# First layer of a four-layer kernel: skip term on TensorE, state faded by GpSimd, last convolution tap by ScalarE

## The reference, cut to what matters

```
zxbcdt = x @ W_in.T                      # z: 512, xBC: 512 + 128 + 128, dt: 64
xBC = silu(causal_conv(xBC, conv_w))     # 4 taps, each channel by itself
dt = softplus(dt_raw + dt_bias); a = dt * -exp(A_log); cum = cumsum(a) in the chunk
Yd = tokens of the same chunk: (C B^T * exp(cum_i - cum_j) * dt_j) @ xs
S_next = S * exp(cum_last) + sum_j exp(cum_last - cum_j) dt_j B_j xs_j
Yoff = exp(cum) * (C @ S)
y = Yd + Yoff + D * xs                   # D: one factor for each head
yz = y * silu(z)
out = (yz * rsqrt(mean(yz^2) + 1e-5) * norm_w) @ W_out.T
```

## Time and profile before

| | |
|---|---|
| runs | 1543.8, 1531.72, 1533.39 us; median 1533.39 us |
| profiled execution | span 1528.5 us from the first to the last instruction; the time of this execution by itself is not listed, the runs shown are 3 to 15 us above the span |
| busy, share of the span | PE 1297.5 us (85%), DVE 916.0 us (60%), ACT 550.5 us (36%), POOL 363.7 us (24%) |
| mean granted TensorE clock | 0.919 of full speed |
| first layer | about 0 to 606 us of the span |

### The profile page before, as it was taken

How to read it: one execution, slowest core, us unless ns; L and a number is a source line. 1 busy time by engine, 2 the same in 40 slices (tenths; PEclk the granted TensorE clock), 3 DMA queues, 4 the chain that set the end, 5 groups by cost and what they waited for, 6 DMA issues and landing times. The chain is left out here.

```text
span 1528.5 us, 21650 instructions
## 1 busy us (share of the span) xinstructions
PE 1297.5 (85%) x7315; PEld 808.2 (53%) x7315; DVE 916.0 (60%) x1809; ACT 550.5 (36%) x917; POOL 363.7 (24%) x346
## 2 busy tenths in 40 slices
PE   5676898898889776889999998999767889999996
PEld 3445545564555455556666745445453456544554
DVE  6776576656675775443312458889877453556344
ACT  2465256635553651222222242442422313233310
POOL 3167113211224142620040002211137000000043
PEclk9886998999899878989999999999958899999998
DMA  9242203220312220400000070000002110112123
GB/s 356 62 114 84 58 24 110 75 67 22 113 41 59 50 91 25 161 11 1 1 0 0 0 248 1 0 1 1 0 19 88 32 31 28 39 39 63 56 62 97
DMA packets 72081, 88.86 MB, mean 58 GB/s; under 512 B 19174, under 2 KB 55334, under 8 KB 71337
## 3 DMA queue, kind: packets, MB, share of 16 engines
q1 hardware_dynamic: 65836, 70.78, 15.1%
q0 software_dynamic: 6144, 16.79, 3.4%
HBM read 61.14 MB, written 26.38 MB: 57 GB/s over the span
## 5 line engine op out<-in xcount | busy, mean ns | idle before, releaser
L397 PE MATMUL l_banks<-l_xnT,all_region_a 128*128 128x512 f32 x288 | 130.2, 605 | 0.0
L913 POOL TENSOR_TENSOR all_region_b<-all_region_b,l_lc 128x512 f32<-128x512 f32 x64 | 89.1, 1412 | 119.8 <-DMA all_region_b<-l_lc_rows 119.5
L1966 PE MATMUL l_banks<-l_xnT,mid_region_c 128*128 128x512 f32 (+1 forms) x192 | 89.4, 615 | 10.8 <-DVE l_xnT L2182 10.8
L397 PEld LDWEIGHTS l_banks<-l_xnT,all_region_a 128*128 128x128 f32 x288 | 54.9, 194 | 62.3 <-issue 61.1
L397 PE MATMUL l_banks<-all_region_b,l_xp 128*32 128x32 f32 x2048 | 35.4, 213 | 48.5 <-DVE all_region_b L1182 43.1
L397 PE MATMUL l_banks<-all_region_a,all_xa 128*128 x234 | 71.6, 436 | 3.8 <-DVEq L1241 2.7
L745 ACT ACTIVATE all_region_b<-all_region_b 128x512 f32<-128x512 f32 x64 | 69.4, 1084 | 4.9 <-PE l_banks L397 0.7
L397 PEld LDWEIGHTS l_banks<-all_region_b,l_xp 128*32 128x32 f32 x2048 | 29.2, 125 | 70.6 <-DVE all_region_b L1182 37.4
L1182 DVE TENSOR_TENSOR all_region_b<-all_region_b,l_cbd 128x512 f32<-128x512 f32 x64 | 56.4, 882 | 16.6 <-ACT all_region_b L745 12.6
L1966 PEld LDWEIGHTS l_banks<-l_xnT,mid_region_c 128*128 128x128 f32 (+1 forms) x192 | 35.1, 188 | 57.1 <-issue 45.3
L2849 POOL TENSOR_TENSOR l_rstd<-l_moments,all_neg_half 128x4 f32<-128x4 f32 x12 | 12.4, 1033 | 219.6 <-DVE l_moments L2909 218.6
(11 more groups left out here) (473 smaller groups left out, 2845.1 us busy)
## 6 DMA issues: line engine op xcount, KB each, us to landing
all_region_b<-l_lc_rows SPq DMA_DIRECT2D x256, 64.0 KB
all_xa<-slots_in SPq DMA_DIRECT2D x39, 128.0 KB, 2.1
slots_out<-all_xa SPq DMA_DIRECT2D x39, 128.0 KB, 1.7
mid_vector_rows<-slots_in SPq DMA_DIRECT2D x39, 128.0 KB, 2.1
slots_out<-all_region_a SPq DMA_DIRECT2D x39, 128.0 KB, 1.7
slots_in<-l_xp SPq DMA_DIRECT2D x4, 1024.0 KB, 12.9
all_region_a<-l_gate_up SPq DMA_DIRECT2D x1, 4096.0 KB, 15.3
all_x<-x SPq DMA_DIRECT2D x4, 512.0 KB, 5.7
```

What stands on the lines that cost most here:

```text
L397: return nc.tensor.matmul(out, lhsT, rhs, start=start, stop=stop, **kw)
L913: nc.gpsimd.tensor_tensor(bc[:, k, :, :], bc[:, k, :, :], spread(lc[:, c, heads], 1, BLK), ALU.subtract).then_inc(dd_ready.sem, 1)
L1966: return nc.tensor.matmul(out, lhsT, rhs, start=start, stop=stop)
```

## The change

It moves work of the first layer between engines and leaves the arithmetic the same but for the order of additions:

- **Last tap.** After evicting a convolution block to `pre`, ACT evicts it a second time into `xbc`, scaled by the last tap's weight; DVE's convolution is then three multiply-adds on top and no first multiplication.
- **Skip term.** ACT makes four diagonal 128x128 matrices of D from the identity once a group (`skips`, in the unused `pre[:, 4]`), behind the wait for the shared expert and ahead of `place`. PE multiplies them with the chunk of `xbc` (`skipped`, four f32 matmuls of 128x128) ahead of strip 1; they open the accumulation in the bank of y, and `assemble` adds to it.
- **Gate.** `take_y` on DVE is one multiplication of the bank by silu(z); GpSimd's `gate` is gone.
- **Fade.** GpSimd multiplies the state by its decay (`fade`), as soon as PE's product with the state is done, ahead of `differences` for the next chunk in its queue. DVE waits for it ahead of the addition.
- ACT waits for the table of columns at its start.

```diff
--- before.py
+++ after.py
@@ -172,6 +172,7 @@
     yg = sb("yg", [P, Z_BLK, P])
     ysq = sb("ysq", [P, Z_BLK, P])
     yr = sb("yr", [P, 2])
+    skip = pre[:, 4, CONV_K - 1:].rearrange("p (k n) -> p k n", k=Z_BLK)
 
     lmax = sb("lmax", [P, TILES])
     steps128 = sb("steps128", [P, TILES])
@@ -291,7 +292,7 @@
     xp_ready = Event(sem("l0_xp_ready"), NCH)
     rw_ready = Event(sem("l0_rw_ready"), NCH)
     yd_ready = Event(sem("l0_yd_ready"), NCH)
-    y_ready = Event(sem("l0_y_ready"), NCH)
+    skip_ready = Event(sem("l0_skip_ready"), 1)
     yg_ready = Event(sem("l0_yg_ready"), NCH)
     ysq_ready = Event(sem("l0_ysq_ready"), NCH)
     ssq_ready = Event(sem("l0_ssq_ready"), NCH)
@@ -299,6 +300,8 @@
     mask_ready = Event(sem("l0_mask_ready"), 1)
     expa_ready = Event(sem("l0_expa_ready"), 1)
     wn_ready = Event(sem("l0_wn_ready"), 1)
+    faded = Event(sem("l0_faded"), 1)
+    fades = [(g, c) for g in range(GROUPS) for c in range(NCH) if (g % HALVES, c) != (HALVES - 1, NCH - 1)]
     zero_ready = Event(sem("l0_zero_ready"), 1)
     ranked = Event(sem("l0_ranked"), 1)
     cleared = sem("l0_cleared")
@@ -314,6 +317,9 @@
     wabs = sb("wabs", [P, 2])
     thr = sb("thr", [P, 2, 2])
     below = pre[:, :, :].rearrange("p j n -> p (j n)")[:, 0:FFN_BLK * DIM]
+
+    def by_head(ap):
+        return ap.rearrange("p (h e) -> p h e", e=HEAD_P)
 
     block = ctx.enter_context(nc.Block())
 
@@ -553,19 +559,28 @@
 
         def assemble(g, c):
 
+            bank = jobs.bank(("y", g, c))
             pe.wait_ge(yd_ready.sem, yd_ready.done(g, c))
-            jobs.wait_room(pe, 0, ("y", g, c))
-            bank = jobs.bank(("y", g, c))
             yout = bank.rearrange("p (k q i) -> p k q i", k=Z_BLK, q=NB)
             for q in range(NB):
                 for m in range(4):
-                    mm(yout[32 * m:32 * m + 32, :, q, :], turn[:, q, :], yd[:, m::4, :], q == 0, False,
+                    mm(yout[32 * m:32 * m + 32, :, q, :], turn[:, q, :], yd[:, m::4, :], False, False,
                        skip_group_check=True)
             pe.wait_ge(yoff_ready.sem, yoff_ready.done(g, c))
             for k in range(Z_BLK):
                 last = mm(bank[:, k * P:(k + 1) * P], yoff[:, k * P:(k + 1) * P], ident[:, :], False, True,
                           skip_group_check=True)
             jobs.fill(last, ("y", g, c))
+
+        def skipped(g, c):
+
+            if c == 0:
+                pe.wait_ge(skip_ready.sem, skip_ready.done(g))
+            jobs.wait_room(pe, 0, ("y", g, c))
+            bank = jobs.bank(("y", g, c))
+            for k in range(Z_BLK):
+                mm(bank[:, k * P:(k + 1) * P], skip[:, k, :], xbc[:, k, c * P:(c + 1) * P], k == 0, False,
+                   skip_group_check=True)
 
         def out_proj(g, c):
 
@@ -645,6 +660,8 @@
             for c in range(NCH):
                 from_before(g, c)
                 for k in range(PIECES):
+                    if k == 1:
+                        skipped(g, c)
                     near(g, c, k)
                     if k == 1 and c + 1 < NCH:
                         by_tokens(g, c + 1)
@@ -683,8 +700,9 @@
             if j < CONV_BLK:
                 if j == 0 and g > 0:
                     act.wait_ge(conv_ready.sem, conv_ready.done(g - 1))
-                nc.scalar.activation(pre[:, j, CONV_K - 1:], jobs.bank(("in", g, j)), ACT.Copy).then_inc(
-                    pre_ready.sem, 1)
+                nc.scalar.activation(pre[:, j, CONV_K - 1:], jobs.bank(("in", g, j)), ACT.Copy)
+                nc.scalar.activation(xbc[:, j, :], jobs.bank(("in", g, j)), ACT.Copy,
+                                     scale=col("conv_w", j * CONV_K + CONV_K - 1)).then_inc(pre_ready.sem, 1)
             else:
                 if j == CONV_BLK and g > 0:
                     act.wait_ge(yg_ready.sem, yg_ready.done(g - 1))
@@ -724,6 +742,15 @@
         def conv_silu(g, j):
             act.wait_ge(conv_ready.sem, conv_ready.done(g, j))
             nc.scalar.activation(xbc[:, j, :], xbc[:, j, :], ACT.Silu).then_inc(xbc_ready.sem, 1)
+
+        def skips(g):
+
+            act.wait_ge(conv_ready.sem, conv_ready.done(g, 4))
+            if g == 0:
+                act.wait_ge(mem.const_ready, mem.n_const)
+            for k in range(Z_BLK):
+                last = nc.scalar.activation(skip[:, k, :], ident[:, :], ACT.Copy, scale=col("D", k))
+            last.then_inc(skip_ready.sem, 1)
 
         def place(g, c):
 
@@ -775,6 +802,7 @@
             nc.scalar.activation(ysq[:, :, :], yg[:, :, :], ACT.Square).then_inc(ysq_ready.sem, 1)
 
         act.wait_ge(mem.l0_row_ready, 16)
+        act.wait_ge(mem.col_ready, 16)
         nc.scalar.activation(exp_a[:, :], row("A_log"), ACT.Exp).then_inc(expa_ready.sem, 1)
         turned("xT", 0, xnT)
         blocks = ((0, 1, 2), (3, 4, 5), (6, 7, 8))
@@ -807,6 +835,7 @@
                     conv_silu(g, 2 * u)
                     conv_silu(g, 2 * u + 1)
             act.wait_ge(hid_ready.sem, hid_ready.done(g, SHARED - 1))
+            skips(g)
             if g == 0:
                 act.wait_ge(cleared, 16 * CLEARS)
             place(g, 0)
@@ -913,13 +942,15 @@
                 nc.gpsimd.tensor_tensor(bc[:, k, :, :], bc[:, k, :, :], spread(lc[:, c, heads], 1, BLK),
                                         ALU.subtract).then_inc(dd_ready.sem, 1)
 
-        def gate(g, c):
-
+        def fade(g, c):
+
+            if (g % HALVES, c) == (HALVES - 1, NCH - 1):
+                return
             if c == 0:
-                pool.wait_ge(z_ready.sem, z_ready.done(g))
-            pool.wait_ge(y_ready.sem, y_ready.done(g, c))
-            nc.gpsimd.tensor_tensor(yg[:, :, :], yg[:, :, :], zs[:, :, c * P:(c + 1) * P], ALU.mult).then_inc(
-                yg_ready.sem, 1)
+                pool.wait_ge(decay_ready.sem, decay_ready.done(g, 2))
+            jobs.wait_filled(pool, 0, ("state", g, c))
+            nc.gpsimd.tensor_tensor(by_head(st[:, :]), by_head(st[:, :]), spread(total[:, c, :], 2, HEAD_P),
+                                    ALU.mult).then_inc(faded.sem, 1)
 
         def scatter(t):
 
@@ -955,6 +986,7 @@
                 for t in range(GT, GT + 2):
                     scatter(t)
             for c in range(NCH):
+                fade(g, c)
                 ahead, behind = late.get(c, ((), ())) if g == 0 else ((), ())
                 if c + 1 < NCH:
                     differences(g, c + 1)
@@ -962,7 +994,6 @@
                         scatter(t)
                 if c > 0:
                     out_scale(g, c - 1)
-                gate(g, c)
                 for t in behind:
                     scatter(t)
             if g == GROUPS - 1:
@@ -1117,12 +1148,13 @@
         def conv(g, j):
 
             dve.wait_ge(pre_ready.sem, pre_ready.done(g, j))
-            nc.vector.tensor_scalar(xbc[:, j, :], pre[:, j, 0:GROUP], col("conv_w", j * CONV_K), None, ALU.mult)
-            for i in range(1, CONV_K):
-                dve.drain()
+            for i in range(CONV_K - 1):
+                if i > 0:
+                    dve.drain()
                 nc.vector.scalar_tensor_tensor(out=xbc[:, j, :], in0=pre[:, j, i:i + GROUP],
                                                scalar=col("conv_w", j * CONV_K + i), in1=xbc[:, j, :],
                                                op0=ALU.mult, op1=ALU.add)
+            dve.drain()
             if g % HALVES == HALVES - 1:
                 nc.vector.memset(pre[:, j, 0:CONV_K - 1], 0.0)
             else:
@@ -1136,9 +1168,6 @@
             nc.vector.tensor_tensor(hT[:, u, :], sg[:, u % 2, :], jobs.bank(("up", g, u)), ALU.mult).then_inc(
                 hid_ready.sem, 1)
             jobs.free(dve.drain(), ("up", g, u))
-
-        def by_head(ap):
-            return ap.rearrange("p (h e) -> p h e", e=HEAD_P)
 
         def take_xs(g, c):
 
@@ -1194,11 +1223,7 @@
             if (g % HALVES, c) == (HALVES - 1, NCH - 1):
                 nc.vector.memset(st[:, :], 0.0).then_inc(state_ready.sem, 1)
                 return
-            if c == 0:
-                dve.wait_ge(decay_ready.sem, decay_ready.done(g, 2))
-            nc.vector.tensor_tensor(by_head(st[:, :]), by_head(st[:, :]), spread(total[:, c, :], 2, HEAD_P),
-                                    ALU.mult)
-            dve.drain()
+            dve.wait_ge(faded.sem, faded.done(fades.index((g, c))))
             jobs.wait_filled(dve, 0, ("next", g, c))
             nc.vector.tensor_tensor(st[:, :], st[:, :], jobs.bank(("next", g, c)), ALU.add).then_inc(state_ready.sem, 1)
             jobs.free(dve.drain(), ("next", g, c))
@@ -1217,12 +1242,10 @@
             if (g, c) != (0, 0):
                 n = g * NCH + c - 1
                 jobs.wait_filled(dve, 0, ("out", n // NCH, n % NCH))
-            bank = jobs.bank(("y", g, c))
-            for k in range(Z_BLK):
-                last = nc.vector.scalar_tensor_tensor(
-                    out=yg[:, k, :], in0=xbc[:, k, c * P:(c + 1) * P], scalar=col("D", k),
```

(6 more changed lines are left out.)

## The result

In ten runs of each on one chip the changed kernel takes 1528.62 us (1521.88 to 1532.9) against 1536.53 (1531.72 to 1546.3): a ratio of 0.9945, 95% interval 0.9923 to 0.9967, some 8 us faster. The forecast was 1549 and slower. The profiled executions span 1520.2 us against 1528.5, with a granted clock of 0.927 against 0.919.

A forecast was written before the change was run, and what follows sets the result against it. PE was taken to bound the projection stretches, with no engine full in the chunk stretches. Terms 3.0 + 2.0 + 9.6 + 0.3 + 0.8 = +15.7 us took the span from 1528.5 to 1544.2, median 1549; range 1521 to 1557.

The forecast's parts named there:

- The clean bursts: At chunk boundaries, fade and four differences on GpSimd hold DVE's strip 1: +9.6 us in groups 1 and 2, +0.3 in 3.
- The three cases: Three clean-starting bursts in the earlier trace where DVE waited for all that was left: 4.17 us at 118.38, 5.10 at 487.47.
- rival 1: At chunk boundaries, GpSimd and DVE still take turns, strip 1 waiting for one difference: +0.6 us, 1534; chance 0.32.
- rival 2: Chain from y to strip 1 gets faster: 0.85 us at each of 10 boundaries, -11 in all, 1522; chance 0.16.
- term of +2.0 in the chunks 3: Skip matmuls on PE ahead of strip 1, half exposed in each chunk 3: 4 x 0.5 = +2.0 us.
- the range: 8 in 10: 1521 to 1557; allows lower PE clock in chunk stretches, four new holes costing another microsecond each.
- Last tap, 0: Moving the convolution's last tap from DVE to ACT is worth nothing, DVE's share falling beside a PE without a gap.
- Diagonals, 1.0 each: ACT's four diagonal matrices ahead of place lie on the path: 1.0 us per group, +3.0 for groups 1 to 3.
- Group 0, +0.8: Chunk 1's fade queues behind scatters, then a clean burst; later scatters shift little: +0.8 us, bounds -1.4 and +5.
- The sum: All terms over the first layer together: +15.7 us, span 1528.5 becoming 1544.2, median 1549.

The follow-up runs named there:

- e4: The changed kernel with ACT's four diagonal matrices made ahead of its wait for the last shared unit: ratio 0.9914 to the kernel before.
- e5: The changed kernel with two indirect DMAs ahead of the fade in chunks 1 and 2 of groups 1 and 2: profile alone, group 0 chunks 86.5 us.
- e6: The changed kernel with three GpSimd powers ahead of the fade in chunks 1 and 2 of groups 1 and 2: profile alone, group 0 chunks 87.9 us.
- e8: The changed kernel with one scatter tile ahead of chunk 1's fade in group 0 and later scatters between the differences: ratio 0.9887 to the kernel before.
- e9: The changed kernel with the fade back on DVE: ratio 0.9991 to the kernel before.
- e11: The changed kernel with a GpSimd drain between fade and differences of chunks 2 and 3 in group 0: profile alone, group 0 chunks 85.7 us.
- e12: The changed kernel with earlier diagonals, group 0's scatters between differences, and a GpSimd drain behind group 3's fetches: ratio 0.9847 to the kernel before.

## Why the prediction was wrong, step by step

- **The clean bursts** (+9.6 in groups 1 and 2, +0.3 in 3): the step that failed, and with it the sign. "Fade and differences become one clean burst" is true; that a clean burst holds DVE is not. It does only straight behind an indirect DMA. At the four boundaries the burst let strip 1 in behind one difference (0.93 us), and strip 2 came 0.95 us earlier on PE where +2.4 was forecast. The three cases were right as measured, but all shared a second condition that I had not looked for. The Trainium skill's rule ("SBUF — State Buffer", on two separate sides), a lock for one instruction, which rival 1 used, fits the bursts without an indirect DMA straight ahead (1.83 us at most); those behind one it does not describe (4.56 us).
- **The boundary without a hold**: rival 2's price of 0.85 us was near; measured 0.95 at strip 2, through the fade on GpSimd (strip 1 1.08 us earlier on DVE, 0.40 of it by the shorter `take_y`, where 0.35 was said). The skip matmuls delay strip 1 on PE by 0.5 us and cost nothing, since strip 2 is the late one; their term of +2.0 in the chunks 3 is not seen, for those chunks only gained. The clock's 1.6 us in group 2 went the other way than the range had it. The fade itself took 1.08 us, not 1.27.
- **Last tap, 0**: wrong. I had read PE's cover off group 1 (42.00 of 42.00) and used it for all groups. In groups 2 and 3 PE waited 0.58 and 1.53 us for the shared unit's product, behind DVE's convolutions. Measured -0.2, -0.8 and -0.8.
- **Diagonals, 1.0 each**: on the path as said, 1.18 each, 1.28 us for the four, which overlap. The Trainium skill's figure ("VectorE: DVE Perf Modes", on the trn2 errata), an estimate of 1.17 us for four, was the better one, though the trace has 0.39 us for a single ACTIVATE and not its 0.29.
- **Group 0, +0.8**: open. The add's wait (4 to 5 us said, 4.34 measured) and the hold at strip 1 came as described; chunk 1's last strip is weighed 1.5 us later by its end, where 2.8 was said. For the whole stretch the traces that share its order of work give +4.1 and +4.4 (changed, e4) and -2.3 and -0.9 (e5, e6), PE's stop being in the first two only. The +0.8 lies between, and no run settles it.
- **The sum**: rival 1's mechanism with rival 2's price in groups 1 to 3, and a group 0 whose size stays open. 1528.6 lies between their 1534 and 1522. In the profile it is -8.3 us against the sum's +15.7: the chunk stretches of groups 1 to 3 make 24.9 us of that difference (-13.0 against +11.9, 1.6 of it the clock), the projection stretches 1.3 and the rest of the span 1.2, and group 0 goes 3.3 us the other way.

## What to carry to other kernels

Before a pattern from three rows becomes a rule, list everything that stands ahead of each case on the same queue and look for a second condition that they share. Keep indirect DMAs on GpSimd away from a run of its SBUF operations that DVE must pass: put idle time, a drain, or the transfers themselves in between; of these the last was timed by itself (e8), the drain only seen to end the hold. A stretch of one trace can differ by 6.7 us between kernels that have nearly the same program there (group 0: 86.5 to 93.2), so look for such repeats before pricing an edit by it. An operation moved to another queue is worth what stands ahead of it there: the same fade costs 11 us behind a gate and scatters and gives some 7 (0 to 14) without the gate.

## What the hardware showed that I had not expected

- Straight behind an indirect DMA (even with a fade of 1.09 us between), GpSimd's run of four differences holds a DVE operation with two SBUF inputs to its end: 4.56, 4.57, 4.57 and 4.58 us, begun 0.9 us into the first difference; 5.43 us when begun 0.05 us into it (e9, at 137.00). Behind idle time or powers: 0.92 to 0.94 at the same distance; behind a drain 1.78 at most. The indirect DMA alone holds nothing: in the changed kernel strip 2 at 121.31, with one of 1.06 us running from 121.16, took 0.69. An operation that runs when the burst starts is held too (6.05 us at 483.03). What inside the chip does this stays open.
- A drain on GpSimd behind indirect DMAs left 1.66 and 0.83 us of gap behind a fade (e11) and 3.54 us behind eight fetches (e12).
- PE's matmuls of one strip (32 records) took 4.5 us instead of 0.63 at the same place in some traces and not in others of the same program (group 0, chunk 2); why is open.
